# Two of 24 FFN hidden chunks threaded through the layer-norm loop ahead of the FFN, in a transformer block on eight cores

## What is computed

```python
x = x + _layernorm(attn(_layernorm(x), Wq, bq, Wk, bk, Wv, bv, Wo, bo))
# ffn, on x of [8, 2048, 1024]; w_gate, w_up [3072, 1024], w_down [1024, 3072]
gate = einsum('bsd,hd->bsh', x, wg)
up = einsum('bsd,hd->bsh', x, wu)
h = silu(gate) * up
x = x + _layernorm(einsum('bsh,dh->bsd', h, wd))   # its input is _layernorm(x)
```

## Time and profile before

| | |
|---|---|
| runs of the kernel before | 1712.28 and 1835.17 us; their median 1773.73 us |
| the profiled execution, its device time | 1710.17 us |
| its span, first to last instruction, slowest core | 1708.6 us |
| spans of the eight cores | 1705.2 to 1708.6 us |
| mean granted TensorE clock | 0.851 to 0.853 on all cores |

### The profile page before, as it was taken

One profiled execution on the slowest core, in us unless ns is written; L12 is line 12 of the kernel. 1 busy time (PEld: TensorE's weight loads), 2 busy tenths in 40 slices (PEclk: granted clock), 3 DMA queues, 4 the chain that ended last, 5 costly groups with the idle time before them and its releaser, 6 DMA issues.

```text
span 1708.6 us, 22327 instructions; the slowest of 8 cores (1705.2 to 1708.6 us)
## 1 busy us (share of the span) xinstructions
PE 1220.3 (71%) x5648; PEld 539.4 (32%) x5648; DVE 524.9 (31%) x1122; ACT 623.9 (37%) x956; POOL 226.3 (13%) x205
## 2 busy tenths in 40 slices
PE   2447776776767777676777912399999999999710
PEld 1123232332322323232323411244444444444310
DVE  4553232231323323133211077612112111000266
ACT  2124545546354464544575334421111111111122
POOL 5102101010110101001000022211111111000022
PEclk9769798897979889797878955599999999999855
DMA  7301101001010000001000300143344335333022
GB/s 89 51 1 19 13 14 13 10 4 16 11 13 13 7 10 10 1 7 13 4 4 13 32 1 1 13 44 38 38 40 42 38 38 50 38 38 37 13 86 98
DMA packets 114633, 43.50 MB, mean 25 GB/s; under 512 B 109264, under 2 KB 109392, under 8 KB 114512
## 3 DMA queue, kind: packets, MB, share of 16 engines
q0 software_dynamic: 111360, 35.66, 18.9%
q1 hardware_dynamic: 2432, 6.29, 1.1%
q10 hardware_dynamic: 720, 0.13, 0.0%
HBM read 63.05 MB, written 8.39 MB: 42 GB/s over the span
## 4 chain that ended last, share of the span: by engine, by line
PE 63%; DVE 17%; ACT 11%; issue 7%; DMA 1%; POOL 1%; DVEq 0%; ACTq 0%; POOLq 0%
PE pS L840 10%; PE pO L851 10%; PE pS L886 10%; PE pS L623 8%; PE pS L377 7%; PE pO L560 7%; ACT s_at L646 5%; DVE s_dmp L245 5%; PE pS L452 3%; PE pS L315 3%; DVE s_dmp L239 3%; ACT s_dmp L509 1%; ACT pO L505 1%; DVE s_at L461 1%; DVE s_b L390 1%
## 5 line engine op out<-in xcount | busy, mean ns | idle before, releaser
L646 ACT ACTIVATE s_at<-pS,s_nB 128x512 bf16<-128x512 f32 (+4 forms) x521 | 349.3, 707 | 312.4 <-PE pS L631 158.3
L623 PE MATMUL pS<-s_b,s_y 128*128 128x512 bf16 (+3 forms) x640 | 227.0, 401 | 29.5 <-ACT s_at L646 13.1
L560 PE MATMUL pO<-s_at,s_b 128*128 128x512 bf16 (+3 forms) x640 | 194.2, 405 | 12.2 <-ACT s_at L646 6.7
L840 PE MATMUL pS<-s_f,s_wb 128*128 128x512 bf16 x768 | 183.2, 382 | 0.0
L851 PE MATMUL pO<-s_f,s_wb 128*128 128x512 bf16 x768 | 181.7, 379 | 0.0
L886 PE MATMUL pS<-s_b,s_wd 128*128 128x512 bf16 x768 | 165.9, 379 | 0.0
L860 ACT ACTIVATE s_dmp<-pS 128x512 bf16<-128x512 f32 x96 | 57.3, 597 | 270.3 <-PE pS L840 270.3
L865 DVE TENSOR_TENSOR s_b<-s_dmp,pO 128x512 bf16<-128x512 bf16 x96 | 66.0, 687 | 267.6 <-PE pO L851 264.5
L377 PE MATMUL pS<-s_f,s_wb 128*128 128x512 bf16 x384 | 123.6, 425 | 15.2 <-DVE s_b L390 8.3
L329 POOL TENSOR_TENSOR s_wd<-s_b 128x512 bf16<-128x512 bf16 x64 | 66.4, 1038 | 404.6 <-DVE s_b L390 359.9
L623 PEld LDWEIGHTS pS<-s_b,s_y 128*128 128x128 bf16 x640 | 69.5, 110 | 125.6 <-issue 90.9
(11 more groups left out here) (91 smaller groups left out, 1287.8 us busy)
## 6 DMA issues: line engine op xcount, KB each, us to landing
s_wb<-wg POOLq DMA_DIRECT2D x24, 256.0 KB, 4.4
s_wb<-wu POOLq DMA_DIRECT2D x24, 256.0 KB, 4.5
s_wd<-wd POOLq DMA_DIRECT2D x8, 768.0 KB, 8.5
s_x<-x POOLq DMA_DIRECT2D x16, 256.0 KB, 7.3
y<-s_y SPq DMA_DIRECT2D x8, 512.0 KB, 2.6
y<-s_y POOLq DMA_DIRECT2D x8, 512.0 KB, 3.0
s_wb<-wq POOLq DMA_DIRECT2D x8, 256.0 KB, 4.5
s_b<-s_dmp SPq DMA_DIRECT2D x16, 128.0 KB, 2.2
```

Of the source, the lines that this page charges most:

```text
L560: e.matmul(pO[:, q0:q0 + n], s_b[:, V0 + 1040 * j + 65 * h: V0 + 1040 * j + 65 * h + 128], s_at[:, 2048 * par + (q0 - 128 * j): 2048 * par ...
L623: e.matmul(pS[:, 512 * sl:512 * sl + n], kpadv[hp][:, 128 * ktc:128 * (ktc + 1)], q_fm(c)[:, q0:q0 + n], start=True, stop=(not diag), skip ...
L646: lambda e, src=src, dst=dst, c=c: e.activation(dst, src, AF.Exp, bias=s_nB[:, c:c + 1], scale=QSCALE),
L840: e.matmul(acc_view(si), wslot(gslot)[:, 128 * kc:128 * (kc + 1)], xfm(kc)[:, 512 * si:512 * (si + 1)], start=first, stop=(kc == ND - 1)),
```

## The change

The four units of chunks 0 and 1 are no longer emitted after the layer-norm loop. Their weight DMAs are emitted ahead of the loop. Whenever the loop has emitted `p3_D` of the fourth tile of a group (t = 6, 10, 14, 18), the unit of that group for chunk 0 and then the one for chunk 1 are pushed on `fifo` as eight pieces each of two matmuls, four for gate and four for up. After each part of a turn (A, B, C, D) one piece is emitted. With the last up piece of a unit come its SiLU and its product. What is left after the loop is drained. The up product goes to bank (si+2)%4 of `pS` for these units, since the loop uses `pO`. The chunks 2 to 23 run as before; `emit_ffn_unit` is the old loop body in a function.

```diff
+    def ffn_dmas(hc):
+        w_chunk_dma(dWg, hc, hc % 2)
+        w_chunk_dma(dWu, hc, 2 + hc % 2)
+
+    def emit_ffn_unit(hc, si):
...
+    def push_ffn_pieces(hc, si):
+        gslot = hc % 2
+        uslot = 2 + hc % 2
+        ub = (si + 2) % 4
+        uview = pS[:, 512 * ub:512 * (ub + 1)]
+        ures = "ps%d" % ub
+        gres = "ps%d" % si
+
+        def gpiece(kc0):
+            for kc in (kc0, kc0 + 1):
+                first = kc == 0
+                op("pe",
+                   lambda e, kc=kc: e.matmul(
+                       acc_view(si), wslot(gslot)[:, 128 * kc:128 * (kc + 1)],
+                       xfm(kc)[:, 512 * si:512 * (si + 1)],
+                       start=(kc == 0), stop=(kc == ND - 1),
+                       skip_group_check=True),
+                   reads=["wb%d" % gslot] + ["ynT%d" % (4 * si + k)
+                                             for k in range(4)],
+                   writes=([gres] if first else []),
+                   bump=([] if first else [gres]))
+
+        def upiece(kc0):
...
+            if kc0 == ND - 2:
+                stg = s_dmp[:, 1024 + 512 * (si % 2): 1536 + 512 * (si % 2)]
+                op("act",
+                   lambda e, stg=stg: e.activation(
+                       stg, acc_view(si), AF.Silu, bias=0.0,
+                       scale=1.0 / 127.0),
+                   reads=[gres], writes=["silu%d" % (si % 2)],
+                   war=(("rrq1", "onq1") if (hc == 0 and si < 2) else ()))
+                op("dve",
+                   lambda e, stg=stg: e.tensor_tensor(
+                       s_b[:, S * hc + 512 * si: S * hc + 512 * (si + 1)],
+                       stg, uview, ALU.mult),
+                   reads=["silu%d" % (si % 2), ures],
+                   writes=["h_%d_%d" % (hc, si)],
+                   war=ffn_hwar(hc) if si == 0 else ())
+
+        for kc0 in range(0, ND, 2):
+            fifo.append(lambda kc0=kc0: gpiece(kc0))
+        for kc0 in range(0, ND, 2):
+            fifo.append(lambda kc0=kc0: upiece(kc0))
+
+    ffn_dmas(0)
+    ffn_dmas(1)
     for t in range(NJ + 3):
         if t < NJ:
             p3_A(t)
+            fifo_step(1)
         if 0 <= t - 1 < NJ:
             p3_B(t - 1)
+            fifo_step(1)
         if 0 <= t - 2 < NJ:
             p3_C(t - 2)
+            fifo_step(1)
         if 0 <= t - 3 < NJ:
             p3_D(t - 3)
-
-    for hc in range(NHC):
...
+            fifo_step(1)
+            if (t - 3) % 4 == 3:
+                si = (t - 3) // 4
+                push_ffn_pieces(0, si)
+                push_ffn_pieces(1, si)
+    fifo_drain()
+
+    for hc in range(2, NHC):
+        ffn_dmas(hc)
         for si in range(4):
...
+            emit_ffn_unit(hc, si)
```

More of the change, by code:

```diff
@@ L810, in p3_D, with ffn_hwar @@
            war=["zf_%d_%d" % (c2, j // 4) for c2 in range(ND)])
+    def ffn_hwar(hc):
+        if hc < ND:
+            return ["zf_%d_%d" % (hc, s2) for s2 in range(4)]
+        if hc < 2 * ND:
+            return ["k_%d_%d" % (hc - ND, s2) for s2 in range(4)]
+        if hc == 2 * ND:
+            return (["vx_%d_%d" % (j2, c2) for j2 in range(NJ)
+                     for c2 in range(ND)] + ["vones"])
+        return []
+    def ffn_dmas(hc):
+        w_chunk_dma(dWg, hc, hc % 2)
+        w_chunk_dma(dWu, hc, 2 + hc % 2)
@@ new lines, in emit_ffn_unit @@
+    def emit_ffn_unit(hc, si):
+        gslot = hc % 2
+        uslot = 2 + hc % 2
+        for kc in range(ND):
+            first = kc == 0
+            op("pe",
+               lambda e, kc=kc, si=si, gslot=gslot, first=first:
+               e.matmul(acc_view(si),
+                        wslot(gslot)[:, 128 * kc:128 * (kc + 1)],
+                        xfm(kc)[:, 512 * si:512 * (si + 1)],
+                        start=first, stop=(kc == ND - 1)),
+               reads=["wb%d" % gslot] + ["ynT%d" % (4 * si + k) for k in range(4)],
+               writes=(["ps%d" % si] if first else []),
+               bump=([] if first else ["ps%d" % si]))
+        for kc in range(ND):
+            first = kc == 0
+            op("pe",
+               lambda e, kc=kc, si=si, uslot=uslot, first=first:
+               e.matmul(pO[:, 512 * si:512 * (si + 1)],
+                        wslot(uslot)[:, 128 * kc:128 * (kc + 1)],
+                        xfm(kc)[:, 512 * si:512 * (si + 1)],
+                        start=first, stop=(kc == ND - 1)),
+               reads=["wb%d" % uslot] + ["ynT%d" % (4 * si + k) for k in range(4)],
+               writes=(["ps%d" % (4 + si)] if first else []),
+               bump=([] if first else ["ps%d" % (4 + si)]))
+        stg = s_dmp[:, 1024 + 512 * (si % 2): 1536 + 512 * (si % 2)]
+        op("act",
+           lambda e, si=si, stg=stg: e.activation(
+               stg, acc_view(si), AF.Silu, bias=0.0, scale=1.0 / 127.0),
+           reads=["ps%d" % si], writes=["silu%d" % (si % 2)],
+           war=(("rrq1", "onq1") if (hc == 0 and si < 2) else ()))
+        op("dve",
+           lambda e, hc=hc, si=si, stg=stg: e.tensor_tensor(
+               s_b[:, S * hc + 512 * si: S * hc + 512 * (si + 1)],
+               stg, pO[:, 512 * si:512 * (si + 1)], ALU.mult),
+           reads=["silu%d" % (si % 2), "ps%d" % (4 + si)],
+           writes=["h_%d_%d" % (hc, si)],
+           war=ffn_hwar(hc) if si == 0 else ())
@@ new lines, in push_ffn_pieces @@
+    def push_ffn_pieces(hc, si):
+        gslot = hc % 2
+        uslot = 2 + hc % 2
+        ub = (si + 2) % 4
[4 more added lines that the diff above has]
+            for kc in (kc0, kc0 + 1):
+                first = kc == 0
+                op("pe",
+                   lambda e, kc=kc: e.matmul(
+                       acc_view(si), wslot(gslot)[:, 128 * kc:128 * (kc + 1)],
+                       xfm(kc)[:, 512 * si:512 * (si + 1)],
+                       start=(kc == 0), stop=(kc == ND - 1),
[5 more added lines that the diff above has]
+        def upiece(kc0):
+            for kc in (kc0, kc0 + 1):
+                first = kc == 0
+                op("pe",
+                   lambda e, kc=kc: e.matmul(
+                       uview, wslot(uslot)[:, 128 * kc:128 * (kc + 1)],
+                       xfm(kc)[:, 512 * si:512 * (si + 1)],
+                       start=(kc == 0), stop=(kc == ND - 1),
+                       skip_group_check=True),
+                   reads=["wb%d" % uslot] + ["ynT%d" % (4 * si + k)
+                                             for k in range(4)],
+                   writes=([ures] if first else []),
+                   bump=([] if first else [ures]))
+            if kc0 == ND - 2:
+                stg = s_dmp[:, 1024 + 512 * (si % 2): 1536 + 512 * (si % 2)]
+                op("act",
+                   lambda e, stg=stg: e.activation(
+                       stg, acc_view(si), AF.Silu, bias=0.0,
+                       scale=1.0 / 127.0),
+                   reads=[gres], writes=["silu%d" % (si % 2)],
+                   war=(("rrq1", "onq1") if (hc == 0 and si < 2) else ()))
+                op("dve",
+                   lambda e, stg=stg: e.tensor_tensor(
+                       s_b[:, S * hc + 512 * si: S * hc + 512 * (si + 1)],
+                       stg, uview, ALU.mult),
+                   reads=["silu%d" % (si % 2), ures],
+                   writes=["h_%d_%d" % (hc, si)],
+                   war=ffn_hwar(hc) if si == 0 else ())
+        for kc0 in range(0, ND, 2):
+            fifo.append(lambda kc0=kc0: gpiece(kc0))
+        for kc0 in range(0, ND, 2):
+            fifo.append(lambda kc0=kc0: upiece(kc0))
@@ L814, in build_program @@
             p3_A(t)
+            fifo_step(1)
         if 0 <= t - 1 < NJ:
             p3_B(t - 1)
+            fifo_step(1)
         if 0 <= t - 2 < NJ:
             p3_C(t - 2)
+            fifo_step(1)
         if 0 <= t - 3 < NJ:
             p3_D(t - 3)
-    for hc in range(NHC):
[L823 to L834, removed]
-        for si in range(4):
[L836 to L870, removed]
```

## The result

| | before | changed |
|---|---|---|
| median of the runs | 1710.96 us (10 runs) | 1724.05 us (12 runs) |
| ratio to before | 1 | 1.0073, 95% interval 1.0062 to 1.0084 |
| span of the profiled execution, slowest core | 1708.6 us | 1722.8 us |
| spans of the eight cores | 1705.2 to 1708.6 us | 1714.7 to 1722.8 us |

The changed kernel is slower by 0.73%, some 13 us: within 2%, beyond its interval, and twice the 6 us that were forecast. (Some executions of every kernel here, the one before among them, run longer with one die at a lower clock; the ratios leave them out, the medians don't, and where they would shift a median much I give the ratio alone.)

What follows compares the result with a forecast made beforehand. VectorE, with ScalarE's Ln and Exp in its chain, was taken to bound the layer-norm loop, and TensorE the FFN. The terms 18.8 - 15.2 + 2.5 = +6.1 us on 1710.17 gave 1716.3 us, range 1700 to 1726.

Steps and rivals of the forecast that it cites:

- chunk 2's weights: After the loop: up is issued only when gate has landed, so TensorE stalls for chunk 2's up weights, +2.5 us.
- the fall of the clock behind the stall: TensorE at chunk 2: clock falling once more at the new stall, 2.1 us, counted only in the range's upper end.
- rival B: Loop and tail: each table load waits for a drain, up to 1.24 us, five times: +6.2, 1722.5 us; chance 0.15.
- What bounds the loop: Layer-norm loop: VectorE is the bound, with ScalarE's Ln and Exp in its chain; added TensorE work is free.
- ScalarE and VectorE, four times: Layer-norm loop: each SiLU and product costs 3.41 us plus 1.29 for the load back, 4.7; four cost +18.8 us.
- Drain at each change of table: ScalarE's table loads: the skill's drain of about 1380 ns per change; four events would cost an estimated 11 us more.
- The tail: Loop's last Identity to chunk 2's first gate matmul: 15.4 us instead of 30.6, a gain of 15.2 us.
- The first four DMAs: Ahead of the loop on GpSimd: first addition at about 987.6, not 985.98; effect between -1.4 and +1.4, taken as 0.

Runs made afterwards that it cites:

- the run with own semaphores: The changed kernel with the weight DMAs of chunks 2 to 23 on four semaphores of their own, so GpSimd no longer waits for the DMA before: 1720.45 us, ratio 1.0051.

## Why the prediction was off

The step that failed is the term for chunk 2's weights. It was put at +2.5 us and measured 4.2, and the fall of the clock behind the stall, another 2.7 us, was left out of the sum. The kernel got slower within 2%, as forecast, but by twice as much: +6.1 against +13 (+14.2 in the profiled spans). That the range of 1700 to 1726 us held 1724.05 was partly luck: most of its upper end came from rival B's drains (+6.2), which did not occur. Step by step:

- *What bounds the loop*: right. VectorE, with Ln and Exp in its chain; the matmuls alone cost nothing.
- *ScalarE and VectorE, four times*: right. 4.7 us an event; measured against the loop without SiLUs it is (146.7 - 127.8) / 4 = 4.7. Both halves, the wait behind L265 and the load back, were taken apart by removing the loads (2.7 us) and by moving product and load (to 0.9).
- *Drain at each change of table* (rival B): not there. The Trainium skill (ScalarE: Activation LUTs, What ACT_TABLE_LOAD costs) adds about 1380 ns of drain to about 1283 ns of load. The five loads of the changed kernel that follow a running Identity start 0.02 us behind its end, and the activation follows 1.29 us later; taking the loop's eight loads away saved 10.8 us, 1.35 each. The Trainium skill's advice to batch by table set (same page, Table sets: the hidden batching unit) holds all the same: these 10.8 us are over half of what the loop had grown by.
- *The tail*: nearly right, -14.1 for -15.2. The low clock at its start came as assumed (granted 0.50 from 1129.3 to 1133.5 us); of the missing 1.1 us a wait for the gate weights is 0.90, which were to land 0.6 us in time.
- *Chunk 2's weights*: the step that failed. Forecast +2.5 us, measured 4.2 + 2.7 = 6.9, and 0.9 in the tail. TensorE and GpSimd there (core 6):

```profile
1143.73 1.89 PE L834 MATMUL pS<-s_f,s_wb 128*128 128x512 bf16 x8 [0.90 <-DMA s_wb<-wg]
1149.66 3.57 PE L845 MATMUL pO<-s_f,s_wb 128*128 128x512 bf16 x8 [4.04 <-DMA s_wb<-wu]
1153.03 2.90 PE L834 MATMUL pS<-s_f,s_wb 128*128 128x512 bf16 x8
1155.77 1.89 PE L845 MATMUL pO<-s_f,s_wb 128*128 128x512 bf16 x8
...
1138.67 0.91 POOL L303 DMA_DIRECT2D s_wb<-wg  x1 [18.51 <-PE pS L892]
1144.64 0.87 POOL L303 DMA_DIRECT2D s_wb<-wu  x1 [5.06 <-PE pS L834]
```

Two faults. First, I took 4.4 us from issue to landing, the median of 24 issues, and 4.8 from issue to issue, from one pair on one core. Here gate was wanted and came 5.06 us after its issue began (1138.67 to 1143.73), GpSimd issued up 5.97 us after gate, and up came after 5.02 more: 11.0 us where 9.3 was reckoned. Over the eight cores it was 9.6 to 11.2. The 5.97 is the landing and 0.91 us more until GpSimd's next issue starts, on every core 0.91 or 0.92; the first issue, too, starts 1.0 us after the last gate matmul of chunk 0 has ended (1135.77 + 1.89), which was put at nothing. (Two sums there are also 0.1 us too high: X + 10.3 with 4.4 and with 4.8 is X + 14.7 and X + 15.1.) A warning stood in the same view of the kernel before, on another core, where the same pair of issues is 5.92 us apart; over the eight cores it is 4.65 to 5.92 (core 0):

```profile
1098.67 0.91 POOL L303 DMA_DIRECT2D s_wb<-wg  x1 [0.33 <-issue]
1104.59 0.87 POOL L303 DMA_DIRECT2D s_wb<-wu  x1 [5.00 <-DMA s_wb<-wg]
```

Second, the fall of the clock behind the stall (4.04 us of waiting, then eight matmuls in 3.57 and eight in 2.90, for 1.89 at full speed) was seen as a possibility and priced at 2.1, but put in the range and not into the sum, for which the prediction gives no reason. The stall was half as long again as forecast, and the clock fell on six of the eight cores. With waits of at most 2.35 us, in the run with own semaphores, it fell on none. The two faults are one chain: a late load, a longer wait, a lower clock.
- *The first four DMAs*: taken as nothing with bounds of 1.4 to either side, measured 1.4 us. The last three issues came 6.85 and 5.84 us apart (again more than 4.8), so the first addition started at 993.56 on this core and not at 987.6. Two additions ran behind each other, and VectorE stood beside them:

```profile
979.98 0.87 POOL L303 DMA_DIRECT2D s_wb<-wu  x1 [3.89 <-DMA s_wb<-wg]
986.83 0.87 POOL L303 DMA_DIRECT2D s_wb<-wg  x1 [5.97 <-PE pO L761]
992.67 0.87 POOL L303 DMA_DIRECT2D s_wb<-wu  x1 [4.97 <-DMA s_wb<-wg]
993.56 4.19 POOL L780 TENSOR_TENSOR s_x<-s_x,s_at 128x1024 bf16<-128x1024 bf16 x2
...
993.30 4.47 DVE L253 TENSOR_TENSOR s_st<-s_st 128x1 f32<-128x1 f32 x1
```

The tiny L253 took 4.47 us on this core; on five others the sum of squares took 5.5 to 6.0. Against that the two passes of 2.6 us in the earlier trace rows are gone, which leaves the 1.4.
- *One core's sum for the slowest of eight*: not reckoned at all. The sum was made on the timeline of one core. The new waits are for DMAs, which differ from core to core (3.25 to 4.04 us for up), and so does what the fallen clock costs: nothing on the cores 0 and 1, 2.7 us on core 6. So the slowest core has 14.2 us where the median of the eight spans, 1718.7 for 1707.9 before, has 10.8. Moving the loads out of the way brought the cores together again.

Of the five places, the stall and the clock of chunk 2 make up 4.4 of the 8 us, the gate weights and the rest of the tail 1.1, the loop 1.8, and the loop's later start on this core 0.7. Of the loop's 1.8 the first loads have 1.4; the remaining 0.4 are not accounted for.

## What to carry to other kernels

Work that is threaded into another loop to fill one engine brings companions on the others, and their place in each engine's order costs more than their length: here four SiLUs and products of 1.3 us busy time cost 4.7 us each as first placed and 0.9 when the product stood one turn later and a tiny activation fetched the table back in idle time. For a load that loses its cover, take the slowest spacing over all cores of the trace and not a median or one core's, and count the clock that falls during the wait. After moving an instruction by half a microsecond, look at what it now runs beside.

## What the runs showed of the hardware

- A VectorE operation with two SBUF inputs that starts beside GpSimd's addition isn't through before the addition has ended, however short it is: L253 on 128x1 took 0.16 us alone, 1.75 and 4.47 beside one and two additions, and ended with them. The sum of squares L245 ended 1.1 us behind the addition (985.98 + 2.11 = 988.09 and 986.55 + 2.63 = 989.18), 1.22 us being its time alone. An L253 that started 0.1 us ahead of the addition kept its 0.16, though the one of 4.47, behind a DMA issue of GpSimd, is recorded 0.26 us ahead of the first of its two; where the limit lies isn't shown. The copies out of PSUM and the product of an SBUF and a PSUM operand kept 0.68 beside one.
- A table load stands behind the wait of its activation (ScalarE was idle for 4.83 us in front of it), so it is on the path of whoever waits for that activation. A tiny activation of the other table, emitted ahead without dependencies, took 1.0 us an event off that path.
- Chunk 2's weight loads of 256 KB in the changed kernel let TensorE go on 4.2 to 5.6 us after the start of their issue, over the eight cores and beside the 4.4 of the page's median; GpSimd's next issue started 0.91 us after that.
- Behind waits of 3.25 to 4.04 us TensorE ran at the low clock on six of the eight cores (granted 0.50 from 1149.66 to 1153.00 us on core 6), but on two, with waits like the others' (3.31 and 3.71 us), it stayed at the full level. What decides between them isn't shown. Behind waits of up to 2.35 us it stayed there on all eight.
